# Rebuilding both ends of a recurrence, and making feed-forward's first norm and half of its first matrix in the last attention body

## What is computed

```
# layer 0: decoder block with cross attention, 16 heads of 32
x = x + attention(ln(x)) @ w_ao                        # self, masked
x = x + attention(ln(x), ctx) @ w_co                   # cross
x = x + gelu(ln(x) @ w1 + b1) @ w2 + b2                # 512 -> 2048 -> 512
# layer 1: RWKV block, 32 heads of 16
xa = ln(x); sx = shift(xa) - xa
t = tanh((xa + sx * maa_x) @ maa_w1)                   # 5 groups of 32
xj = xa + sx * (maa_j + t_j @ maa_w2_j)                # j = w, k, v, r, g
w = exp(-exp(time_decay + tanh(xw @ decay_w1) @ decay_w2))
r, k, v, g = xr @ Wr.T, xk @ Wk.T, xv @ Wv.T, silu(xg @ Wg.T)
for each token: out = r . (faaaa * k v + s);  s = k v + w * s
x = x + (groupnorm(out) * g) @ Wo.T
xc = ln(x); k2, r2 = mixes of xc and its shift
x = x + sigmoid(r2 @ fWr.T) * (relu(k2 @ fWk.T) ** 2 @ fWv.T)
```

## Time and profile before

| | |
|---|---|
| time, median of 3 runs (lowest, highest) | 4081.64 us (4079.44, 4081.74) |
| time of the profiled execution / its span | 4082.07 / 4079.9 us |
| busy share: TensorE, VectorE, ScalarE, GpSimd | 90%, 72%, 50%, 45% |
| mean granted TensorE clock | 0.948 of 2.4 GHz |
| attentions, phase_b, phase_c: from | 0, 1516.0, 2285.7 us |
| one steady feed-forward item | 45.3 us, TensorE busy all of it |
| one steady recurrence body | about 103 us |
| first scan; last scan's end | 2375.1; 4009.4 us |

### The profile page before, as it was taken

The page is one execution under the profiler, slowest core; times in us unless marked ns, Lnnn a source line. Parts: engine busy times, 40 slices in busy tenths (PEclk is TensorE's granted clock), DMA queues, the critical chain, the costliest instruction groups (busy, mean ns, idle before and its releaser), DMA issues. The chain is left out here.

```text
span 4079.9 us, 71207 instructions
## 1 busy us (share of the span) xinstructions
PE 3690.2 (90%) x21637; PEld 2818.7 (69%) x21637; DVE 2953.4 (72%) x6718; ACT 2035.7 (50%) x5168; POOL 1846.5 (45%) x1265
## 2 busy tenths in 40 slices
PE   7999999899999978999999678999999999999976
PEld 6777777777777757999999555666565566656643
DVE  6778777888888866556655357777778777777773
ACT  5777777777777755455555312333333333333321
POOL 5444444644444430000000146666666666666662
PEclk9999999999999989999999788999999999999988
DMA  5344444544444432010001200000000000000000
GB/s 149 98 108 112 98 103 109 144 124 110 116 122 122 126 98 76 31 46 31 31 31 46 103 14 19 24 25 24 25 24 25 24 25 24 25 24 24 19 19 16
DMA packets 144450, 256.58 MB, mean 63 GB/s; under 512 B 25024, under 2 KB 29888, under 8 KB 143264
## 3 DMA queue, kind: packets, MB, share of 16 engines
q1 hardware_dynamic: 144288, 254.50, 22.9%
HBM read 107.61 MB, written 33.55 MB: 35 GB/s over the span
## 5 line engine op out<-in xcount | busy, mean ns | idle before, releaser
L434 POOL TENSOR_TENSOR a_prob<-a_prob,a_rsums 128x512 f32<-128x512 f32 x512 | 539.5, 1055 | 781.9 <-DVE a_rsums L612 781.8
L1374 POOL TENSOR_TENSOR c_S<-c_S,c_rT 128x1024 f32<-128x1024 f32 x256 | 603.6, 2358 | 323.6 <-DVE c_S L1693 323.6
L506 ACT ACTIVATE a_prob<-a_t,a_tmin 128x256 f32<-128x256 f32 x1024 | 512.6, 501 | 367.3 <-DVE a_tmin L605 366.1
L1693 DVE TENSOR_TENSOR_SCAN c_S<-c_wT,c_vb 128x512 f32<-128x512 f32 x512 | 625.1, 1221 | 44.6 <-issue 2.7
L1688 DVE TENSOR_TENSOR c_vb<-c_kT,c_vb 128x510 f32<-128x510 f32 x512 | 351.3, 686 | 294.1 <-PE c_vb L1884 271.6
L601 DVE SCALAR_TENSOR_TENSOR a_ps_s<-a_ps_s,a_mask 128x512 f32<-128x512 f32 x512 | 357.4, 698 | 180.7 <-PE a_ps_s L702 112.5
L605 DVE CUSTOM_DVE_ANT_0 a_t<-a_ps_s,a_mneg 128x256 f32<-128x256 f32 x1024 | 394.2, 422 | 60.1 <-issue 0.7
L712 PE MATMUL a_ps_t<-w_ident,a_prob 128*128 128x128 f32 x2048 | 323.5, 282 | 27.3 <-ACT a_probT L516 18.0
L1884 PE MATMUL c_vb<-c_vhl,c_spread 128*128 128x512 f32 x512 | 296.2, 588 | 45.7 <-DVE c_S L1693 33.2
L976 PE MATMUL b_ps<-b_ln_high,b_w_high 128*128 128x256 f32 x1024 | 290.9, 284 | 17.6 <-DVE b_ln_low L918 17.6
L702 PE MATMUL a_ps_s<-a_stack 96*128 96x256 f32 x1024 | 230.3, 307 | 82.4 <-DMA a_stack<-a_parts_qk 65.3
(11 more groups left out here) (232 smaller groups left out, 9582.6 us busy)
## 6 DMA issues: line engine op xcount, KB each, us to landing
a_stack<-a_parts_qk SPq DMA_DIRECT2D x768, 128.0 KB, 2.4
w_x_in<-x SPq DMA_DIRECT2D x48, 512.0 KB, 3.9
x<-a_xb SPq DMA_DIRECT2D x32, 512.0 KB, 2.8
w_x_in<-in_x SPq DMA_DIRECT2D x16, 512.0 KB, 3.6
a_xb<-in_x SPq DMA_DIRECT2D x16, 512.0 KB, 3.6
a_enc<-in_ctx SPq DMA_DIRECT2D x16, 512.0 KB, 4.4
a_xb<-x SPq DMA_DIRECT2D x16, 512.0 KB, 3.6
b_shared<-in_w SPq DMA_DIRECT2D x16, 512.0 KB, 4.6
```

Of the source, the lines that this page charges most:

```text
L434: nc.gpsimd.tensor_tensor(prob[:, h % 4, :, :], prob[:, h % 4, :, :], rsums[:, h, :].unsqueeze(2).to_broadcast([P, TC, T]), ALU.mult).then ...
L506: op = nc.scalar.activation(prob[:, n % 4, tc, :], t[:, n % 2, tc, :], ACT.Exp, bias=tmin[:, n, tc:tc + 1], scale=-1.0, accum_out=psums[:, ...
L1374: nc.gpsimd.tensor_tensor(S[:, n % 4, :, :], S[:, n % 4, :, :], rT[:, par, :, :], ALU.mult).then_inc(z_ready, 1)
L1693: nc.vector.tensor_tensor_scan(flat(pair(S[:, n % 4, :, :], i)), flat(pair(wT[:, par, :, :], i)), flat(x), 0.0, ALU.mult, ALU.add).then_in ...
```

## The change

*In attentions*: w_q and w_k are laid into the memory of a new pair w1_first (high and low half of w1's first 1024 columns), which lives on through the feed-forward. In the last body with heads (31), steps 4 to 11, ScalarE casts an eighth of it a step and VectorE subtracts it a step later; its stages are the free buffers raw and enc. The same body norms x of feed-forward's item 0. SP issues the load of that x and four loads of w1 before second_pair of body 31.

*In phase_b*: only w1's second half is split before item 0's gelu; w2's pieces are split one to a gelu unit of item 0, through x4, xb, x_in and one shared slot. Item 0 stands outside the loop, transposes don't wait for a norm, and the last item norms x of item 0 for phase_c.

*In phase_c*: body -2 has no ln1. VectorE makes its shift and xxx, and in body -1 the additions of xaT (k before w) and the product r k. The bias rows are made by one-row matmuls with the identity and copied by VectorE. SP loads Wk right after same_head. Constants on TensorE and ScalarE's rearrangement of Wv move to step 4 of body -1. KEEP names steps at which TensorE makes matmuls that nobody reads: 4 in body -2; 14, 6 and 5 in body -1; 8, 20, 8, 16 and 20 in the last body, where TensorE first waits for the last scan.

```
-                second_pair(2 * B - 1)
                 sp.wait_ge(filled, units.filled(2 * B - 1, "lnT1"))
                 sp.dma_start(x_in[:, :, :], x3_d[0]).then_inc(dsem["x_next"], 16)
+                for c in range(KC):
+                    if c == 3:
+                        sp.wait_ge(filled, units.filled(2 * B - 1, "encT1"))
+                    sp.dma_start(w1_stage(c), ...).then_inc(w1_loaded[c], 16)
+                second_pair(2 * B - 1)
...
+                        for i, high, _, whole in w1_eighths(k, n):        # scalar
+                            act.wait_ge(filled, units.filled(k + 1, "k3"))
+                            act.wait_ge(w1_loaded[i // 2], 16)
+                            nc.scalar.copy(high, whole).then_inc(w1_high, 1)
...
+                        for i, high, low, whole in w1_eighths(k, n - 1):  # vector
+                            dve.wait_ge(w1_high, i + 1)
+                            nc.vector.tensor_tensor(low, whole, high, ALU.subtract)
...
-                for i, (src, _) in enumerate(pieces):                     # phase_b, sync
-                    if i >= 4:
-                        sp.wait_ge(weight_split, i - 3 if i in W1 else i - 2)
+                    if i == KC + 2:
+                        sp.wait_ge(filled, units.filled(0, "lnT1"))
+                    if i == KC + 3:
+                        sp.wait_ge(ln_split, 2)
+                    if i >= KC + 4:
+                        sp.wait_ge(weight_split, i - 3)
...
+                sp.wait_ge(weight_split, len(pieces))
                 with sp.Fori(0, B - 1) as it:
...
+                            if first(it) and i == 0:                      # scalar, item
+                                for j in W1:
+                                    high_part(j)
+                                act.wait_ge(weight_split, len(W1))
...
+                            if first(it):
+                                high_part(W2[i])
...
-                    if not last:                                          # vector, item
-                        normalise(it + 1)
+                    normalise(it + 1)
...
+                def first_shift(k):                                       # phase_c, vector
+                    dve.wait_ge(emptied["act"], units.emptied(k + 2, "xaT1"))
+                    nc.vector.tensor_tensor(sx[:, :, :], xaT[:, :, 0:T], xaT[:, :, 1:T + 1], ALU.subtract)
+                    nc.vector.drain()
+                    for c in range(KC):
+                        op = nc.vector.scalar_tensor_tensor(xmix[:, 0, c, :], sx[:, c, :], col(w["cols"], "maa_x", c),
+                                                            xaT[:, c, 1:T + 1], ALU.mult, ALU.add)
+                    op.then_inc(xxx_ready, 1)
...
+                        if before(k, 0) and i == 1 and what != "mw":      # vector, read
+                            nc.vector.drain()
+                            for m in ("k", "w") if what == "mk" else what[1]:
+                                xj = xmix[:, (MIX.index(m) + 1) % 2, :, :]
+                                nc.vector.tensor_tensor(xj, xj, xaT[:, :, 1:T + 1], ALU.add).then_inc(xj_ready, 1)
...
+                def keep_clock(n):                                        # tensor
+                    for _ in range(n):
+                        nc.tensor.matmul(vb[:, 2, 0:P], w["ident"][:, :], w["ident"][:, :], start=True, stop=True)
...
+    KEEP = {-2: {14: 4}, -1: {2: 14, 6: 6, 8: 5}, B: {1: 8, 4: 20, 5: 8, 8: 16, 11: 20}}
...
+                        if last(k) and n == 1:
+                            pe.wait_ge(scanned, k * 2 * RS)
+                        if before(k, 0) or last(k):
+                            keep_clock(KEEP[k].get(n, 0))
```

More of the change, by code:

```diff
@@ L776, in phase_b @@
         w1_d, w2_d = [d[n].rearrange("(c p) n -> p c n", p=P) for n in ("w1", "w2")]
-        HALF = FF // 2
-        pieces = [(w1_d[:, c, half * HALF:(half + 1) * HALF], [x[:, c, half * HALF:(half + 1) * HALF] for x in w1_parts])
-                  for half in range(2) for c in range(KC)]
+        pieces = [(w1_d[:, c, HALF:FF], [x[:, c, :] for x in w1_parts[1]]) for c in range(KC)]
         pieces += [(w2_d[:, 2 * i:2 * i + 2, :],
@@ L783, in phase_b, with first, before_first @@
                    for i in range(FC // 2)]
-        W1, W2 = range(2 * KC), range(2 * KC, 2 * KC + FC // 2)
+        W1, W2 = range(KC), range(KC, KC + FC // 2)
         def stage(i):
-            return shared[:, i % 4 + (1 if i in W2 else 0), :]
+            if i in W1:
+                return shared[:, 1 + i, :]
+            return [flat_parts(x4), flat_parts(xb), flat_parts(x_in), shared[:, 0, :]][i % 4]
+        def first(it):
+            return isinstance(it, int) and it == 0
+        def before_first(it):
+            return isinstance(it, int) and it < 0
         with nc.Block() as block:
@@ L835, in _, with high_part @@
                                         ALU.add).then_inc(xb_ready, 1)
+                inverse_deviation(B)
             @block.scalar
             def _(act):
[L839 to L843, removed]
+                def high_part(i):
+                    act.wait_ge(weights_loaded[i], 16)
+                    nc.scalar.copy(pieces[i][1][0], stage(i)).then_inc(weight_high, 1)
                 act.sem_inc(emptied["act"], units.per["act"] + NU)
@@ L956, in item @@
                     dve.sem_inc(x4_ready, 1)
-                normalise(0)
-                low_parts(W1)
                 split_lnT(-1)
-                low_parts(W2)
-                with dve.Fori(0, B - 1) as it:
+                for i in W1:
+                    low_part(i)
+                item(0, False)
+                with dve.Fori(1, B - 1) as it:
                     item(it, False)
@@ L1204, in iterations @@
         def iterations(engine, body):
-            body(-2, ("ln1", "norm", "t"), 0)
+            body(-2, ("norm", "t"), 0)
             body(-1, ("front", "ln1", "norm"), 1)
@@ L1377, in body @@
                             back(k, n, 1 - par)
-                        if n == (RK_0 if first(k) else AT["rk"]) and "front" in parts:
+                        if n == (RK_0 if first(k) else AT["rk"]) and "front" in parts and not before(k, 0):
                             pool.wait_ge(emptied["act"], table_of(k).emptied(k + 2, "r1"))
@@ L1381, in body @@
                                                     ALU.mult).then_inc(rk_ready, 1)
-                        if "front" in parts:
+                        if "front" in parts and not before(k, 0):
                             for name, at in zip(MIX, ADD_XA_0 if first(k) else ADD_XA):
@@ L1386, in body @@
                         if "ln1" in parts and n == step_of(k, "ln1_root"):
-                            inverse_deviation("ln1", k + 3)
-                        if "norm" in parts:
+                            inverse_deviation("ln1", k + 2)
+                        if "norm" in parts and not before(k, -1):
                             if n == AT["sx"]:
@@ L1912, in body @@
                         take(k, fills_of(k, n)[1], parts, par)
-                    if isinstance(k, int) and k == -2:
-                        constants()
+                        if "front" in parts and before(k, 0) and n == 4:
+                            constants()
                 iterations(pe, body)
@@ L1934, in build_program @@
         d["x4"] = nc.dram_tensor("x4", (B, T, C), F32, kind="Internal").ap()
-        attentions(nc, d, w, dsem)
-        phase_b(nc, d, w, dsem)
+        with ExitStack() as first:
+            w["w1_first"] = [first.enter_context(nc.sbuf_tensor("w1_first_" + n, [P, KC, FF // 2], F32R)) for n in ("high", "low")]
+            attentions(nc, d, w, dsem)
+            phase_b(nc, d, w, dsem)
         phase_c(nc, d, out, w, dsem)
```

154 lines of the change are left out of this document (102 added, 52 removed).

## The result

The changed kernel takes 4056.27 us (median of 4, 4054.49 to 4060.24) against 4081.63: ratio 0.9943, interval 0.9930 to 0.9955, so about 23 us faster (the medians differ by 25). Forecast was 4040. Both are cut at the same events: GpSimd's first instruction of the recurrence, the first broadcast, and VectorE's reads of the accumulator (one a body, in the body after the scans of its item).

A forecast was written before the change was run, and what follows sets the result against it. TensorE, busy nine tenths of the span, was taken as the bound, with three stretches below full clock: feed-forward's start, recurrence's start and end. 2 - 13.7 - 23 - 7.5 = -42 from 4081.64 gave 4040 us, range 4032 to 4056.

The forecast's parts named there:

- A: Last attention body: added w1 splitting and a norm, mostly covered by VectorE's waits; +2 us, from 0 to +6.
- B: Feed-forward's start: fewer w1 pieces, norm and W2 splits ahead of the first product; item 1 starts 13.7 us sooner.
- C: Recurrence's start: norm gone, work moved to VectorE, matmuls kept warm; first broadcast 23 us sooner, bounds -17 and -25.
- the steady bodies' periods rose: Sign of being wrong: recurrence's steady bodies, forecast to change by 0, would show longer periods.
- step (5): Recurrence's start: k's and w's xaT add on VectorE; k starts at 2306.7 for 2322.64, less 14 fillers, 0.5 sticking out.
- D: Last recurrence body: 72 fillers hold TensorE's clock for faster products; -7.5 us, or +1.5 if the clock doesn't hold.
- groups of 20 ... in gaps of 6.20 and 6.23 before zT and kk: Last body: two groups of 20 fillers, 5.1 us warm or 9.4 cold, would fit their gaps if warm.
- the rest only for its period: Outside feed-forward's start and the recurrence's start and end, only the period was read; steady bodies forecast at 0.
- Rival 4: Slower: thirteen steady bodies lie otherwise to the clock; at 4 us a body +10, 4092; chance 0.04, half of it slower.
- rival 3: Recurrence's earlier start not taken up, through late weight loads or body 0's pacing; its gain falls to -8, 4055; chance 0.04.
- rival 2: Feed-forward gain swallowed: units of 5 us and attention +6 from port and ScalarE; -28, 4054; chance 0.06.
- rival 1: Fillers don't hold the clock: last body +1.5, recurrence's start loses 3; -30, 4052; chance 0.13.

The follow-up runs named there:

- a_unroll: Changed kernel with the loop over recurrence bodies 1 to 12 written out, no jump back on any engine: 4050.7 us, ratio 0.9928.
- u_no11: Changed kernel with that loop written out and the 20 fillers of step 11 in the last body taken out: 4045.0 us, ratio 0.9916.
- l_best: Changed kernel, loop kept, with 28 semaphore increments in body 0 and last-body fillers moved directly behind zT's and xcT's transposes: 4036.8 us, ratio 0.9891.

## Why the prediction was off

The direction was right, and of the four edits A, B and C worked as described; 4040 was 16 us too low, just outside the range (4056). One of the prediction's own signs of being wrong came true: the steady bodies' periods rose.

- **A** (+2): VectorE's last read of the attentions moves from 1511.92 to 1514.12, +2.2. Right, and for the reason given: six of the eight low halves start ahead of GpSimd's multiply, or without one, and take 0.67 or 0.68 us; two start 0.1 and 0.2 us behind it and take 1.50 and 1.41.
- **B** (-13.7): the opening of the recurrence shows A and B together at -16.9, -14.6 as a mean over the eleven profiles that have this code (2268.3 to 2272.7) and three that have the old one (2284.2 to 2285.7); forecast -11.7. B alone is then about -19 in this pair of profiles and -17 as a mean. Units were 3.63 and not 3.8, transposes for item 1 began 47.8 us after the stage's opening and not 52, and these eight took 1.06: the clock held where I had it fall. The period of the items behind is 45.72 in both kernels, so unmoved as assumed (the 45.3 of the table before is 0.4 too low).
- **C** (-23): measured -17.9. Each step's work went as described, but t starts 10.8 us after the opening for 9.1, and **step (5)'s "14 fillers, 0.5 of which stick out"** failed: I priced them at the 2.4 GHz rate, and the clock had fallen to 1.2 just ahead of them (2287.30 to 2294.13). They stick out by 3.7. Where it didn't fall, in a_unroll and u_no11, the first broadcast gains 22.2 and 22.3 of the 23, with t as late as here (a_unroll), so most of the miss in C is this one group at this clock. k, r and v start 11.5, 14.1 and 17.1 us sooner from the opening, for 16, 19 and 22.
- **D** (-7.5): failed in size and sign, +1.6. The step is **"groups of 20 ... in gaps of 6.20 and 6.23 before zT and kk"**: I read the gap and the size of the group, and not where in TensorE's queue the group stands to the wait that makes the gap. The first of the two lies ahead of its wait and filled it; the second lies behind. The terms themselves were near: transposes gained 0.9 each for 0.5, and Wo and fWk took 7.1 for 6.9. Counted from the last read, I had zT, Wo, fWk and fWr start 1.6, 2.1, 4.4 and 7.3 us sooner; in l_best, where every group stands ahead of its wait, they start 1.6, 2.1, 4.2 and 6.8 sooner (9.64, 13.65, 33.43 and 40.42 for 11.28, 15.74, 37.62 and 47.23). In the changed kernel the late groups give back 1.9 at Wo and, with fWr at 49.14, 8.7 in all.
- **The steady bodies** (0): the largest error, +10.0, and **"the rest only for its period"** is the step. I took code that isn't edited as unmoved. Rival 4 had the place (the steady bodies) but the wrong cause: the clock's part is the same 0.95 to 0.96 before and after, and instructions added ahead of the loop remove the 10 us again. What the runs showed in its place is the wait for a block of code at each of five jumps, 12.3 us in all.
- Body 0 let the gain through (rival 3 falls), units didn't run at 5 (rival 2 falls), the clock was held for most products (rival 1 falls by its own words, though k's fillers met the low clock, and its price, -30 with nothing gained at the end, is near the -25 that happened).

Without the 9.1 us missed in D and the 10.0 in the loop it would have been 4056.3 - 19.1 = 4037, near the 4040; the 5 us missed in C and the 5 won in B cancel.

## What to carry to other kernels

A loop body that nobody touched can slow down because code ahead of it grew: compare the periods that hold a jump with those that don't, look for TensorE idle on "issue" there that ends just behind a 16 KB instruction fetch, and if it is there, shift the loop by a few dozen instructions placed in a wait, or write it out, before judging the edit. Fillers that are to bridge a wait belong in the queue directly behind the last work, ahead of every wait that ends with the gap, and must be priced at the clock that holds when they start. A filler group that is too long costs its whole excess, so compare with no fillers at all.

## What was unexpected of the hardware

- The stall at a jump back depends on where its target lies: 0 us (shifts of +28, +32, +64 instructions), 2.2 to 2.9 at the changed kernel's place, 0.7 to 1.5 at -16, 1.2 to 1.8 in the kernel before with 15 more, 0 to 0.4 without. It ends 1.2 to 1.6 us after the second of two 16 KB fetches has landed, at all fifteen jumps that stall.
- VectorE's own stall at the same jumps is 3.3 to 3.6 us in all looped kernels but the changed one, where VectorE's idle time there (3.64 us at the first jump) is put down to the late broadcast. No run here tells what it costs.
- One semaphore increment on TensorE took 0.14 us at the start of a stage (64 of them moved the next matmul by 9.1 us), and nothing visible in a wait of body 0.
- The same code ahead of it opened the recurrence anywhere between 2268.3 and 2272.7 us, and 21 runs of the kernel before spread over 4075.3 to 4087.6, so 1 or 2 us can't be read from a median here; the stretches of a profile can tell them.
